# Adding an output bias to the residual rows in DRAM instead of in the matmul, and moving two gathered pairs, in a one-core GNN, attention and mixture-of-experts layer

## What is computed

```python
xn = LN(x)
h   = xn * rsqrt(deg_out)                       # graph branch
agg = segment_sum(h[src], dst) * rsqrt(deg_in)
gnn = l2_normalize(relu(agg @ W + b))
q, k, v = split(xn @ w_qkv.T)                   # linear attention, 8 heads of 64
k, v = instance_norm(k), instance_norm(v)
mix = ((q @ (k.T @ v)) / N) @ w_out.T + b_out   # per head
x = x + gnn + mix
x = x + moe(LN(x))                              # 8 experts, top 1, capacity 977
```

## Time and profile before

| | |
|---|---|
| median of 3 runs | 1450.29 us (1450.14 to 1451.77) |
| the profiled execution | 1450.29 us |
| its span, first to last instruction | 1449.1 us |
| mean granted clock of TensorE, as a share of 2.4 GHz | 0.971 |
| busy, share of the span: PE, DVE, ACT, POOL | 90%, 83%, 64%, 55% |
| moved by DMA | 132.91 MB, 92 GB/s on average |

### The profile page before, as it was taken

The page is one execution under the profiler, slowest core; times in us unless marked ns, Lnnn a source line. Parts: engine busy times, 40 slices in busy tenths (PEclk is TensorE's granted clock), DMA queues, the critical chain, the costliest instruction groups (busy, mean ns, idle before and its releaser), DMA issues. The chain is left out here.

```text
span 1449.1 us, 38869 instructions
## 1 busy us (share of the span) xinstructions
PE 1308.9 (90%) x14100; PEld 1095.7 (76%) x14102; DVE 1196.2 (83%) x2460; ACT 934.0 (64%) x2122; POOL 796.1 (55%) x622
## 2 busy tenths in 40 slices
PE   4788889995889999999998999999898998999987
PEld 3455555563769888888888888988895787889986
DVE  7887878988869889998989889998975586767776
ACT  4577777777546666666676766667663657464744
POOL 6545545206238888888888885000000577776574
PEclk9899999997989999999999999999999999999999
DMA  9111111003826555555656554111123443353220
GB/s 299 54 33 44 42 40 35 28 30 123 232 58 128 103 100 97 99 99 109 133 97 131 105 100 82 38 66 46 38 74 103 127 136 107 100 158 96 75 76 25
DMA packets 94847, 132.91 MB, mean 92 GB/s; under 512 B 14038, under 2 KB 72046, under 8 KB 94657
## 3 DMA queue, kind: packets, MB, share of 16 engines
q0 software_dynamic: 44640, 63.45, 22.4%
q1 hardware_dynamic: 50032, 67.20, 14.0%
HBM read 92.27 MB, written 47.33 MB: 96 GB/s over the span
## 5 line engine op out<-in xcount | busy, mean ns | idle before, releaser
L1673 PE MATMUL bank<-reg_b,reg_a 128*128 128x256 f16 x4410 | 592.8, 273 | 8.0 <-ACT reg_a L1262 5.9
L1262 ACT ACTIVATE reg_a<-bank 128x392 f16<-128x392 f32 x720 | 342.3, 496 | 213.2 <-PE bank L1665 182.6
L961 POOL DMA_INDIRECT reg_a<-h_rows,reg_d x216 | 396.9, 1837 | 66.5 <-issue 65.5
L1673 PEld LDWEIGHTS bank<-reg_b,reg_a 128*128 128x128 f16 x4410 | 394.9, 98 | 49.5 <-issue 10.1
L1950 DVE TENSOR_TENSOR reg_c<-iota_v,reg_c 128x2048 f16<-128x2048 f16 (+1 forms) x282 | 368.1, 1321 | 34.1 <-PE bank L1665 16.0
L1665 PE MATMUL bank<-reg_a,reg_c 128*128 128x98 f16 x2880 | 241.8, 209 | 16.5 <-ACT reg_a L1262 7.9
L1665 PEld LDWEIGHTS bank<-reg_a,reg_c 128*128 128x128 f16 x2880 | 199.3, 99 | 31.6 <-issue 17.1
L1950 DVE TENSOR_TENSOR reg_a<-iota_h,reg_c 128x1568 f16<-128x1568 f16 x180 | 174.2, 968 | 0.0
L975 POOL COPY take_idx<-inv_i 128x8 int32<-128x8 int32 (+1 forms) x8 | 1.7, 214 | 229.7 <-DVE inv_i L2508 229.7
L1906 PE MATMUL bank<-w_hi,hid_hi 128*128 128x256 f32 (+1 forms) x368 | 108.6, 295 | 11.4 <-DVE w_lo L2543 7.1
L1908 PE MATMUL bank<-w_hi,hid_lo 128*128 128x256 f32 (+1 forms) x368 | 105.8, 288 | 0.0
(11 more groups left out here) (378 smaller groups left out, 2535.9 us busy)
## 6 DMA issues: line engine op xcount, KB each, us to landing
reg_b<-in_L_ffn_w SPq DMA_DIRECT2D x16, 1024.0 KB
h_rows<-reg_b POOLq DMA_DIRECT2D x14, 896.0 KB, 10.0
tok_rows<-reg_e SPq DMA_DIRECT2D x24, 512.0 KB
x_t<-in_x SPq DMA_DIRECT2D x24, 256.0 KB
xnT_t<-xnT_rows SPq DMA_DIRECT2D x24, 256.0 KB
out<-reg_e SPq DMA_DIRECT2D x24, 256.0 KB
reg_a<-h_rows,reg_d POOLq DMA_INDIRECT x224
xnT_rows<-xnT_t SPq DMA_DIRECT2D x13, 256.0 KB
```

The source lines that it names most:

```text
L961: ins = g.indirect_dma_start(out=acc[i % 2][m][k], out_offset=None, in_=h_rows, in_offset=at, compute_op=ALU.add)
L1262: return a.activation(AT[k].rearrange("p h (w t) -> p h w t", w=2)[:, :, :, s * GROUP:(s + 1) * GROUP], tile_ps[bk][:, 0:GROUP * 2 * NB].r ...
L1673: ins = t_.matmul(agg_ps[k][:, 0:D], AT[k][:, h, :], h_all[:, half, h, :], start=(first and h + half == 0), stop=(last and h == NB - 1 and ...
```

## The change

The bias is added to x instead. SP copies x in DRAM to x_bias in one DMA and makes five copies of b_out; POOL adds them to x_bias with ten adding DMAs of 625 rows, one ahead of every fifth fetch from the 16th on. The loads of x for the finishing read x_bias, after a wait for all ten. The matmul with b_out_at, its operands and what prepares them are gone. Besides, GATHERED becomes (8, 16); by finish_starts() the gathered pairs then start at slots 296 and 520.

```diff
+XB_ROWS = 250
+XB_JOIN = 5
+XB_PARTS = 10
+XB_FROM = 3
-GATHERED = (9, 18)
+GATHERED = (8, 16)
@@ SP
         sp.dma_start(wq[:, :, :], wv[:, 0:IC, :]).then_inc(w_in2, 16)
+        sp.dma_start(x_bias.rearrange("(p j) d -> p (j d)", p=XB_ROWS), x.rearrange("(p j) d -> p (j d)", p=XB_ROWS)
+                     ).then_inc(xb_in, 16)
+        sp.dma_start(b_out_rows, b_out.rearrange("(a d) -> a d", a=1).to_broadcast([XB_JOIN, D])).then_inc(xb_in, 16)
         sp.dma_start(gate_w_sb[:, :, :], gate_w.rearrange("(c p) d -> p c d", p=P)).then_inc(w_in2, 16)
...
-            sp.dma_start(x_t[:, :, :], pair_rows(x, q)).then_inc(x_ld, 16)
+            sp.dma_start(x_t[:, :, :], pair_rows(x_bias, q)).then_inc(x_ld, 16)
...
         sp.wait_ge(hw_ready, NB)
+        sp.wait_ge(xb_set, 16 * XB_PARTS)
         load_pair(0)
@@ POOL
+        def bias_rows(n):
+            if n == 0:
+                pool.wait_ge(xb_in, 32)
+            rows = N // XB_PARTS
+            part = x_bias[n * rows:(n + 1) * rows, :].rearrange("(p j) d -> p (j d)", j=XB_JOIN)
+            b_rows = b_out_rows.rearrange("(a j) d -> a (j d)", a=1).to_broadcast([rows // XB_JOIN, XB_JOIN * D])
+            g.dma_start(part, b_rows, accum_op=ALU.add).then_inc(xb_set, 16)
         def pace():
             q, i = divmod(n_paced[0], G_PAIR)
             if i == 0:
                 pool.wait_ge(hot_used, HBUF + HFIRST + HBUF - 1 + HBUF * q)
+            if i == 0 and XB_FROM <= q < XB_FROM + XB_PARTS:
+                bias_rows(q - XB_FROM)
...
-        chain(g.memset(b_out_at, 0.0))
-        for half in range(2):
-            chain(g.memset(b_out_at[half * 64:half * 64 + 1, :], HSCALE))
@@ PE
-                    t_.matmul(o.mix_ps[:, m, :], b_out_at, b_out_hl, start=True, stop=False)
-                    ins = thirds(o.mix_ps[:, m, :], m, lambda l, c: mix_hl[:, l, c, 0:D], o.xnT, True)
+                    ins = thirds(o.mix_ps[:, m, :], m, lambda l, c: mix_hl[:, l, c, 0:D], o.xnT)
@@ DVE
-                link(v_.tensor_tensor(mix_inv[:, 0:D], b_out_bc[:, :], b_out_bc[:, :], ALU.mult))
-                v_.tensor_scalar(mix_bc[:, D:DG], mix_n2[:, D:DG], TINY, None, ALU.max)
-                v_.scalar_tensor_tensor(mix_bc[:, 0:D], mix_n2[:, 0:D], TINY, mix_inv[:, 0:D], ALU.max, ALU.add
-                                        ).then_inc(mix_prep, 1)
+                v_.tensor_scalar(mix_bc[:, :], mix_n2, TINY, None, ALU.max).then_inc(mix_prep, 1)
...
-                link(v_.tensor_tensor(b_out_bc[:, :], b_out_bc[:, :], mix_inv[:, 0:D], ALU.mult))
-                link(v_.tensor_scalar(b_out_hl, b_out_bc[:, :], HSCALE, None, ALU.mult))
-                low = slice(64, P)
-                v_.scalar_tensor_tensor(b_out_hl[low, :], b_out_bc[low, :], HSCALE, b_out_hl[low, :], ALU.mult, ALU.subtract)
```

More of the change, by code:

```diff
@@ L107 @@
 XB = 6
-GATHERED = (9, 18)
+XB_ROWS = 250
+XB_JOIN = 5
+XB_PARTS = 10
+XB_FROM = 3
+assert N % (XB_JOIN * XB_PARTS) == 0 and XB_JOIN * D <= 2048
+GATHERED = (8, 16)
 GB = 2 * len(GATHERED)
@@ L148, in build @@
     tok_rows = dram("tok_rows", (NPAD, TOKW))
+    x_bias, b_out_rows = dram("x_bias", (N, D)), dram("b_out_rows", (XB_JOIN, D))
     h_rows = dram("h_rows", (NPAD, D))
@@ L247, in build @@
     slot_src = reg_d[:, 0:NB * SLOT].bitcast(I32).rearrange("p (b j) -> p b j", b=NB)
-    o = NB * SLOT
-    b_out_at, b_out_hl = reg_d[:, o:o + P // 2].bitcast(F16), reg_d[:, o + P // 2:o + P // 2 + D // 2].bitcast(F16)
-    assert o + P // 2 + D // 2 <= 3328
     wkv_nat = reg_e[:, 0:2048].rearrange("p (c d) -> p c d", c=8)
@@ L428, in build @@
         "mix_hi", "mix_set"))}
-    x_ld, xT_ld = sem("x_ld"), sem("xT_ld")
+    x_ld, xT_ld, xb_in, xb_set = sem("x_ld"), sem("xT_ld"), sem("xb_in"), sem("xb_set")
     fin_dve, fin_scaled = sem("fin_dve"), sem("fin_scaled")
@@ L687, in pair_rows @@
             if blocks_of(q) == 1:
-                n = LAST if rows is x or rows is out else P
+                n = LAST if rows is x_bias or rows is out else P
             rows = rows[ds(first, n), :]
@@ L727, in _ @@
         sp.wait_ge(agg_done, NB - 1)
-        sp.dma_start(last_fin.x[0:LAST, 0, :], pair_rows(x, NQ)).then_inc(x_ld, 16)
-        sp.dma_start(last_fin.x[LAST:P, 0, :], x[0:P - LAST, :]).then_inc(x_ld, 16)
+        sp.dma_start(last_fin.x[0:LAST, 0, :], pair_rows(x_bias, NQ)).then_inc(x_ld, 16)
+        sp.dma_start(last_fin.x[LAST:P, 0, :], x_bias[0:P - LAST, :]).then_inc(x_ld, 16)
         last_T = xnT_rows[NQ * P:(NQ + 1) * P, :].rearrange("p (l m d) -> p l m d", l=2, m=2)
@@ L1534, in _, with thirds @@
         HALVES = ((0, 0), (0, 1), (1, 0))
-        def thirds(out_ps, m, right, left=xnT_t, begun=False):
+        def thirds(out_ps, m, right, left=xnT_t):
             for n, (lx, lw) in enumerate(HALVES):
                 for c in range(DC):
-                    ins = t_.matmul(out_ps, left[:, lx, m, c * P:(c + 1) * P], right(lw, c), start=(n + c == 0 and not begun),
+                    ins = t_.matmul(out_ps, left[:, lx, m, c * P:(c + 1) * P], right(lw, c), start=(n + c == 0),
                                     stop=(n == 2 and c == DC - 1))
```

## The result

The changed kernel takes 1466.89 us (median of 13 executions, 1459.72 to 1472.56), the kernel before, run beside it, 1452.94 us (13 executions, 1449.30 to 1462.71). The ratio is 1.0083, 95% interval [1.0062, 1.0103]: slower by 12 us (the medians differ by 14.0), where 5.5 were forecast and 1464 was the upper end of the range. The direction was right, the size was not. The profiled execution took 1463.94 us; its span is 1462.7, 13.6 more than the one of before.

The account below looks back on a forecast made before the run. PE was taken to bind the aggregation. Copy +3.0, additions +0.5 and aggregation +2.0 (matmuls' gain included) gave +5.5 on 1450.3: 1455.8 us, with an 8-in-10 range of 1447.5 to 1464.

Parts of the forecast that it names:

- The copy: SP's queue in the K/V phase: copy delays the first xnT_rows store, ACT stands 3.9 to 6.8 us; +3.0 us net.
- ACT's slack: K/V phase: idle time on PE and ACT after the stall takes in some 2 us of it.
- Rival 3: Copy on SP's queue runs over 10 of 16 engines, 25 us, ACT stands 13 us: 1464 us; chance 0.1.
- The additions: Ten adding DMAs on POOL's queue, about 90 to 190 us: +0.5 us, bounds 0 and +8.
- The matmuls: Aggregation: 49 removed matmuls each hold PE 0.11 us, a gain of 5.4 us, bounds 13.3 and 0.
- PE binds: Aggregation, about 350 to 1100 us: PE busy 98%, DVE 90%, so PE time removed counts as real gain, -5.4 us.
- The gathered sums: Slots 296 and 520: DVE waits about 5.5 us, then stands 7.3 us later; aggregation with the matmuls' gain +2.0 us.
- relu's 1 us and the four tile banks' 4 us: Second gathered pair: slack between DVE and PE that leaves +2.3 us of DVE's 7.3 us lag.
- pinned at 897.1: Aggregation, slot 520: DVE cannot pass before 897.1 us whatever was gained, so PE's earlier 3.5 us are lost.

Follow-up runs that it names:

- b_copy: Kernel before plus the copy of x to x_bias and the b_out rows on SP's queue, nothing reading x_bias: 1414.78 us against 1408.02, ratio 1.0052.
- a_again: The changed kernel, unaltered, measured again against the kernel before: 1424.09 us against 1408.96, ratio 1.0115.
- a_late_918: Changed kernel with gathered pairs back at 9 and 18 and the copy in ten parts behind stores: 1411.81 us; kernel before 1409.03, ratio 1.0027.
- b_816_third: Kernel before with only the gathered pairs moved to 8 and 16, third measurement: 1418.22 us against 1408.96, ratio 1.0064.
- b_copy_add: Kernel before plus the copy and the ten additions, results unused, matmuls and pairs 9 and 18 kept: 1450.72 us against 1446.58, ratio 1.0022.
- a_same: The changed kernel, unaltered, measured beside the kernel before: 1458.00 us against 1446.58, ratio 1.0069.

## Why the prediction was wrong

Forecast 5.5 = 3.0 + 0.5 + 2.0; the two profiled executions differ by 13.6, of which 6.5 stand at the end of the K/V phase and 7.1 come after it. At the last relu of the aggregation the changed kernel is 15.1 us late; what follows gives 1.5 back, about what that stretch differs by between traces on this kind of chip (340.3 to 342.0 us).

**The copy: right in its mechanism, too small by 3.5 us.** The prediction had the store landing at 56.1 to 59.0 and ACT standing 3.9 to 6.8 us; it stood 10.35. The trace's DMA records have the copy as 128 descriptors of 50,000 bytes, 16 in the works at once from 40 to 52 us. A piece took 2.29 us on average, and 2.38 where it ran wholly between 40 and 52: 16 x 50,000 / 2.38 = 336 GB/s, a little under the lower of the two rates that were taken. But the first piece began at 34.7 us and the last ended at 59.1: 24.4 us, not 18.3 (8 rounds of 2.29). One piece was in the works at 36 us and 13 at 38; the copy of src ran until 37.8, ahead of it in the queue. 6 were left at 56 us and 2 at 58: they didn't finish together. The store landed behind the last. The sum took the rate of full engines, with no slow start and no tail. Where a trace tells the landing of that store, it is 60.8 us (b_copy) and 61.8 (a_again) behind the copy and 41.7 and 41.8 without it (a_late_918, b_816_third): 19 to 20 us later, where the sum had 15.6 to 18.5. ACT's slack gave back 3.9 us, not 2. Net 6.5 against 3.0; the upper bound of the term was 6.8.

Rival 3 (ten engines, 25 us) gave nearly this length of the copy, for another reason: sixteen descriptors at once, at a DMA share of 0.98 to 1.18 of all 16 engines between 40 and 52 us, speak against ten engines. The Trainium skill (DMA: Bandwidth & Descriptors, "Why a DMA increments its semaphore by 16 and not by 1") would give ten for 250 rows, and adds that software can split a contiguous pattern anew. The 128 pieces of 50,000 bytes, which aren't the 250 rows of 25,600 that the kernel names, are such a split.

**The additions: right.** 0.5 forecast; a_again shifts by 0.4 us while they run, and b_copy_add costs no more than b_copy.

**The matmuls: the step "PE binds" failed.** It rested on PE at 98% busy and DVE at 90%. A matmul's printed time is 272 ns and the next starts after 110, so of a pause behind one the first 0.16 us count as busy; and the 2% that were left are one pause a pair. From start to start, that gap is 0.65 us beyond the usual spacing in the kernel before, 0.88 in the changed one, 0.44 with twice the matmuls, 0.29 with eight: up to twice, each two matmuls change it by their own 0.22 us, and a pair stays at 31.1 to 31.4 us (one of the changed kernel's at 31.76). The saving was lost at a hand-over from DVE. In the sum this was worth less than 5.4, since it had already given up 3.5 us at slot 520: 1.9 us.

**The gathered sums: right that the waits come, wrong in how they reach PE.** The prediction had DVE standing 5.5 us at the first place and 7.3 us late at the second (waits of 3.2 and 4.5 us were seen behind the copy's shift, 7.7 and 3.0 in b_816_third), of which relu's 1 us and the four tile banks' 4 us would be absorbed. It followed DVE's queue to chunks and to relu. Nearer stands `choose` of the pair in front, and PE's mix step waits for that: 6.85 us of 7.7 came through in b_816_third, and in the changed kernel 1.0 of 3.2 at the first place and 3.7 of 4.5 at the second. The traces and the code show this wait. Taking the sums behind `choose` brought +9.3 down to +3.9, which agrees; but the same edit gives the gathers four slots, some 4 us, more, so how much of the gain is the order alone isn't separated. Two of its arguments were wrong in a smaller way: the phase isn't pinned at 897.1, since POOL's gathers start with the aggregation (419.5 us before, 425.4 after; the last is issued at 891.6 and 895.9), so that the wait comes on top of the shift; and with a shorter wait on DVE than predicted PE was later than predicted. Without the matmuls' gain the prediction had 2.3 + 1.6 = 3.9 us here, and 7.1 were seen after the K/V phase. PE's waits for `choose` are 4.7 of them; the rest isn't located.

Together: 3.5 (copy) + 1.9 (matmuls) + 3.2 (sums) - 0.5 (additions) = 8.1, and 5.5 + 8.1 = 13.6. The third of these is what the others leave over, so that the sum comes out is no proof of it.

**Open.** What sets 31.15 us a pair: neither PE's nor DVE's own work, and not the hand-over of add_slots alone; a ring of hand-overs between them is argued, not shown. What makes the stretch between the last low_T and the first relu 68 us long in one trace and 75 in another. Why one kind of chip ends the K/V phase 30 us earlier. No version beat the kernel before by more than the noise.

## What to carry to other kernels

A busy share near 100% doesn't say that an engine sets the pace when its operations overlap: look from start to start for one pause per period, and before counting a removed operation as gained, see whether it stands ahead of such a pause. When an engine will have to wait, list everything behind it in its queue and take the first item that another engine needs, not the ones that look largest. A large transfer ahead of a small store in one queue delayed it here until the last piece was through; issued in parts behind the stores, the same bytes cost 2.8 us instead of 7 to 9. And when an edit costs a few microseconds, compare the traces stage by stage first: a stage that the edit doesn't touch may differ by as much.

## What the runs showed of the hardware

A copy of 6.4 MB from DRAM to DRAM had 16 pieces in the works from 40 to 52 us, at 336 GB/s by their mean of 2.38 us, but took 24.4 us from the first piece to the last, so 262 GB/s. A load of 128 KB issued right behind it landed 26.5 us after its issue instead of 6.2. The same kernel takes 1446 to 1453 us on some chips and 1408 to 1409 on others, most of the difference in one phase: between two traces of the changed kernel (a_same and a_again) 30.2 of 36.1 us stand at the end of the K/V phase.
